# The first normalised tile of an attention and mixture-of-experts kernel: turned by DMA instead of by TensorE

## The chip, the cores and the metric

The kernel runs on one core of one Trainium2 chip. The metric is the time of one execution on the device, in microseconds. Five engines run their own instruction streams and meet only at semaphores: TensorE (PE), VectorE (DVE), ScalarE (ACT), GpSimd (POOL), and SyncE (SP), which here only issues DMA transfers.

## The reference

Layer norm, cross-attention to a short context, layer norm, and a feed-forward block with eight experts and a shared one, both added to their input:

```python
x = x + _L0_xattn_ref(_layernorm(x), ctx_512, Wq, Wkv_expand, Wout)
x = x + _L0_ffn_ref(_layernorm(x), router_w, wg, wu, wd, sg_w, sg_b, su_w, su_b, sd_w, sd_b)
# attention: 16 heads of 32, 64 keys per batch, masked where the key index is above the query's
# feed-forward: two experts per token, chosen and weighted by the router's scores,
#   y = sum over the two of score * (silu(x @ wg) * (x @ wu)) @ wd, plus the shared expert with biases
```

x is 8 batches x 512 tokens x 512, float32.

## The kernel before

The 4096 tokens are T = 32 tiles of 128, four to a batch. The kernel has a fill (loading and scaling of weights, mixed with the first tiles), the passage of the 32 tiles through attention, the shared expert over 32 tiles, and the experts over 71 slots of gathered tokens. The change is in the fill and the passage.

Every matrix that TensorE multiplies is split into two float16 parts, a high and a low one, and a product is three passes (high-high, high-low, low-high). ScalarE makes the high part with a scaled copy, and VectorE or GpSimd the low part as the difference to what was copied.

The passage is a software pipeline. `step(b, j)` on every engine works on tile 4b + j and on the tiles up to six behind it (t1 to t6): first layer norm of the tile itself, turning it (t1), product by w_q and scores (t2), probabilities times values (t3), projection by w_o, residual and second layer norm's statistics (t4), second normalised tile xn2 (t5), router (t6). The order of instructions on each engine is written out by hand in these step functions; nothing reorders them, so an instruction that waits holds all behind it on its engine. The batches 3 to 7 run in a hardware loop; the rest is unrolled. After the last tile six more steps (`LAG`) drain the pipeline, and the shared expert's entries are woven into them (`entry_amid`).

In such a step of tile n, the first layer norm goes: statistics on VectorE (L1057, L1062, `ln_var`); the variance chain `inv_std` on GpSimd, three one-column instructions L566, L569, L573, whose last releases `ln_rstd`; the activation L850 on ScalarE, which writes the float32 tile `xn1` (one buffer). In the step after, TensorE turns xn1 with four float32 transposes into a PSUM bank (`turn_first`, L1417), ScalarE copies the high part into `xn1T` and VectorE makes the low part (`turn_first` in each of them). The second normalised tile goes another way already: ScalarE writes xn2 (L840) and the high part of `xn2p`, GpSimd subtracts the low part (L643), and SP issues a DMA transpose of both into `xn2T` (L446).

Beside this, from batch 2 on, ScalarE and GpSimd split the experts' weights in pieces of 512 columns: ScalarE writes the high part and a scaled float32 copy `piece` (one buffer), and GpSimd subtracts (L580). The steps j = 0, 2 and 3 of a batch have two pieces each, j = 1 has none, but has `batch_keys` on GpSimd (L609, four copies that follow one another); j = 3 has `batch_values` (L617). GpSimd also adds a bias to the residual tile (L668) and joins the router's logits (L659). The splits of w_o, w_r and the shared expert's weights are made in steps 3 to 9 (`more_weights`), the values of the context in pairs of batches (`VALUE_PAIRS`).

Of the kernel before, what the change touches and what calls it, by code (L numbers as in the profile page):

```python
# [25 lines left out]
F16 = mybir.dt.float16  # L26
# [6 lines left out]
P = 128  # L33
# [48 lines left out]
VALUE_PAIRS = ((0, 6, 0), (3, 0, 2), (1, 2, 4), (2, 2, 6))  # L82
VALUE_PARTS = 8
# [5 lines left out]
def xattn_moe(nc, x, ctxT, wqT, wkT, wvT, woT, routerT, experts, shared, sh_b, sd_b, out):  # L89
# [5 lines left out]
    with stack:  # L95
# [70 lines left out]
        silu_g = sb("silu_g", [P, I])  # L166
        hid = sb("hid", [P, I])
# [11 lines left out]
        sums_out = hidT[:, 2:4, :, :, :].rearrange("p n v c q -> p (n v c q)")  # L179
# [58 lines left out]
        def flat(t4):  # L238
# [23 lines left out]
        xn1_ready, xn1T_mm, xn1T_hi, xn1T_ready, q_mm, qT_hi, qT_ready = [sem(n) for n in (  # L262
            "xn1_ready", "xn1T_mm", "xn1T_hi", "xn1T_ready", "q_mm", "qT_hi", "qT_ready")]
# [30 lines left out]
        wo_scaled, wsh_scaled = sem("wo_scaled"), sem("wsh_scaled")  # L294
# [63 lines left out]
        def value_banks(n):  # L358

            first = VALUE_PAIRS[n][1]  # L360
            return (first, first + 1)

        def value_parts(v, n):


            a, z = value_banks(n)
            b = 2 * VALUE_PAIRS[n][0]
            blocks = ((b, a, 2),) if z == a + 1 else ((b, a, 1), (b + 1, z, 1))
            for h in range(2):
                rows = slice(SK * h, SK * h + SK)  # L370
                for first, at, k in blocks:
                    yield rows, v_all[rows, v, first:first + k, :, :], psum[rows, at:at + k, :].rearrange(
                        "p b (r h d) -> p b r h d", h=2, d=HD)[:, :, :, h, :]
# [5 lines left out]
        def _(sp):  # L379
# [28 lines left out]
            def step(b, j):  # L408
                tile = TPB * b + j
                t3, t5, t6 = tile - 3, tile - 5, tile - 6  # L410
# [4 lines left out]
                if live(t3):  # L415
                    load_again(t3, j + 1)
                if live(t6):
# [7 lines left out]
                if j == 2 and isinstance(b, int) and b == 2:  # L425
                    sp.wait_ge(wsh_split, 7)
                    sp.wait_ge(wo_split, 4)
                    sp.wait_ge(wq_split, 2)
                    sp.wait_ge(k_split, 1)
                    sp.wait_ge(v_split, VALUE_PARTS)  # L430
# [1279 lines left out]
```

## Time and profile before

| | us |
|---|---|
| runs | 803.75 median of 3 (800.55 to 804.62) |
| profiled execution | 802.11 |
| its span (first to last instruction) | 800.4 |
| TensorE busy in the span | 762.3 (95%) |
| VectorE, ScalarE, GpSimd busy | 578.3, 459.9, 432.5 |
| first step with pieces to the drain | about 111 to 320 |
| one batch of the loop | 38.0 |

The granted clock of TensorE is a mean of 0.993 of full speed. In a timeline, each row has a start, a duration, the engine, the source line of the profiled kernel, what is written and read with shapes, a count, and, where the engine had been idle before, for how long and who released it. A row of the table by stretch has the stretch, its length, the busy time (and instructions) of PE, PEld (TensorE's weight loads), DVE, ACT and POOL in this order, the granted clock, the busy share of the DMA engines and GB/s. Consecutive equal instructions may be merged into one row. Durations can overlap a little: the next instruction of an engine may start before the last one's end.

### The profile page before, as it was taken

Reading aid. Unit: us, or ns where it says so; the run is one execution under the profiler, and the core shown is the slowest. Engines: PE = TensorE matmul, PEld = TensorE weight load, DVE = VectorE, ACT = ScalarE, POOL = GpSimd, SP = SyncE. Lnnn points to the kernel's source line nnn. Section 1 sums busy time; section 2 is a strip of 40 time slices with the busy share of each in tenths; the row PEclk is TensorE's granted clock in tenths of the full one; section 3 lists DMA queues with packets and bytes.
Section 4 is the critical chain, followed back from the end, with each engine's and each line's share of the span. In section 5 each row is a group of like instructions: output and inputs, shape, how many; then the busy total and the mean of one; then the engine's idle time right before and its main releaser. Section 6 shows DMA issues by size and latency. Waiting matters only on the chain.

```text
span 800.4 us, 21951 instructions
## 1 busy us (share of the span) xinstructions
PE 762.3 (95%) x7249; PEld 522.4 (65%) x7249; DVE 578.3 (72%) x1188; ACT 459.9 (57%) x846; POOL 432.5 (54%) x562
## 2 busy tenths in 40 slices
PE   4888999999999999889999999999999999999995
PEld 2766888888888888668888874455555555555552
DVE  5988999999999898646788685555555565555553
ACT  4777889989888989575546433333333333333330
POOL 3335787777777777444110202655655556556543
PEclk9999999999999999999999999999999999999998
DMA  8325768677766767647856655989898989989892
GB/s 289 121 66 173 205 204 233 191 230 210 207 205 199 215 205 216 200 134 247 266 172 215 195 186 131 138 149 147 145 156 147 160 144 153 152 134 165 145 146 35
DMA packets 138318, 140.73 MB, mean 176 GB/s; under 512 B 87872, under 2 KB 88896, under 8 KB 137856
## 3 DMA queue, kind: packets, MB, share of 16 engines
q1 hardware_dynamic: 122336, 104.01, 47.5%
q0 software_dynamic: 15904, 35.70, 25.6%
q8 instruction: 47, 0.77, 0.4%
q14 instruction: 31, 0.25, 0.1%
HBM read 71.61 MB, written 52.31 MB: 155 GB/s over the span
## 4 chain that ended last, share of the span: by engine, by line
PE 79%; DMA 3%; ACT 1%; issue 1%; POOL 1%; DVE 1%; SPq 0%; POOLq 0%; ACTq 0%
PE psum L1426 45%; PE psum L1489 18%; PE psum L1417 9%; PE psum L1541 4%; PE psum L1580 2%; DMA hidT<-xn2p 1%; DMA out<-w_q,tabs 1%; DMA probsT<-normed_turned 0%; DMA xn1T<-normed_turned 0%; PE psum L1559 0%; PE psum L1601 0%; PE psum L1562 0%; PE psum L1544 0%; ACT attnT L747 0%; ACT xn L840 0%
## 5 line engine op out<-in xcount | busy, mean ns | idle before, releaser
L727 POOL DMA_INDIRECT out<-w_q,tabs x71 | 112.5, 1584 | 108.6 <-DVE w_q L1406 74.3
L717 POOL DMA_INDIRECT x_in<-normed_tokens,tabs x71 | 70.5, 993 | 91.2 <-DVE tabs L1287 42.2
L922 ACT ACTIVATE silu_g<-psum,tabs 128x256 f32<-128x256 f32 x71 | 33.6, 473 | 146.0 <-PE psum L1426 137.8
L1391 DVE SCALAR_TENSOR_TENSOR hid<-psum,tabs,silu_g 128x256 f32<-128x256 f32 x71 | 34.4, 484 | 111.3 <-ACT silu_g L922 111.3
L1426 PE MATMUL psum<-exp_all,hidT 128*128 x426 | 103.4, 379 | 1.7 <-DMA hidT<-xn2p 1.5
L1426 PE MATMUL psum<-exp_all,probsT 128*128 x420 | 96.4, 379 | 0.0
L1426 PE MATMUL psum<-w_o,attnT 128*128 128x512 f16 x384 | 89.7, 384 | 1.6 <-DVE attnT L1111 1.6
L1489 PE MATMUL psum<-xn1T,w_q 128*128 128x128 f16 x1536 | 91.0, 219 | 0.0
L1489 PEld LDWEIGHTS psum<-xn1T,w_q 128*128 128x128 f16 x1536 | 86.3, 98 | 0.7 <-issue 0.6
L580 POOL TENSOR_TENSOR exp_all<-piece,exp_all 128x512 f32 (+1 forms) x48 | 56.2, 1170 | 43.9 <-ACT piece L747 43.9
L1426 PEld LDWEIGHTS psum<-exp_all,hidT 128*128 128x128 f16 x426 | 41.7, 98 | 52.3 <-issue 3.4
L1426 PEld LDWEIGHTS psum<-exp_all,probsT 128*128 128x128 f16 x420 | 41.1, 98 | 41.9
L1406 DVE TENSOR_SCALAR w_q<-psum,y_w 128x512 f32<-128x512 f32 x71 | 53.3, 751 | 20.2 <-PE psum L1426 16.7
L1426 PEld LDWEIGHTS psum<-w_o,attnT 128*128 128x128 f16 x384 | 35.6, 98 | 40.9 <-issue 2.2
L747 ACT ACTIVATE probsT<-psum 128x512 f16<-128x512 f32 x99 | 55.6, 601 | 8.2 <-PE psum L1417 8.0
L1541 PE MATMUL psum<-kv_store,qT 128*128 128x256 f16 x384 | 48.5, 273 | 5.9 <-issue 4.0
L747 ACT ACTIVATE xn2p<-hid 128x256 f16<-128x256 f32 x70 | 29.2, 417 | 38.6 <-DVE hid L1391 37.5
L1426 PE MATMUL psum<-exp_all,qT 128*128 x216 | 49.6, 379 | 0.0
L1426 PE MATMUL psum<-exp_all,xn1T 128*128 x216 | 49.6, 379 | 0.0
L1489 PE MATMUL psum<-probsT,w_sh 128*128 128x128 f16 x768 | 45.8, 219 | 2.4 <-DMA probsT<-normed_turned 1.7
L1489 PEld LDWEIGHTS psum<-probsT,w_sh 128*128 128x128 f16 x768 | 43.8, 98 | 5.0 <-issue 2.9
L1426 PE MATMUL psum<-w_sh,hidT 128*128 128x512 f16 x192 | 46.7, 379 | 0.0
(213 smaller groups left out, 1645.0 us busy)
## 6 DMA issues: line engine op xcount, KB each, us to landing
x_in<-x SPq DMA_DIRECT2D x64, 256.0 KB, 3.0
exp_all<-experts SPq DMA_DIRECT2D x24, 512.0 KB, 5.1
out<-xy SPq DMA_DIRECT2D x32, 256.0 KB, 3.3
normed_tokens<-xn SPq DMA_DIRECT2D x32, 256.0 KB, 4.8
normed_turned<-xn2T SPq DMA_DIRECT2D x32, 256.0 KB, 3.4
w_q<-out SPq DMA_DIRECT2D x32, 256.0 KB, 2.8
out<-w_q SPq DMA_DIRECT2D x32, 256.0 KB, 2.1
probsT<-normed_turned SPq DMA_DIRECT2D x16, 256.0 KB, 3.3
```

What stands on the lines that cost most here:

```text
L580: pool.tensor_tensor(split_piece(e, 1, k), piece[:, :], split_piece(e, 0, k), ALU.subtract).then_inc(piece_split, 1)
L717: pool.indirect_dma_start(x_in[:, t % 4, :], None, xn_dram, bass.IndirectOffsetOnAxis(gather_at[:, t:t + 1], 0)).then_inc(gathered[t % 4], 16)
L727: pool.indirect_dma_start(out, bass.IndirectOffsetOnAxis(add_at[:, t:t + 1], 0), y[:, t % Y_RING, :], None, bounds_check=TOKENS - 1, oob_i ...
L747: act.activation(dst, src, ACT.Copy, scale=scale).then_inc(done, 1)
L922: act.activation(silu_g[:, :], psum[:, GU_BANK[m % 2], 0:I], ACT.Silu, scale=gate_scale_at[:, tm:tm + 1]).then_inc(silu_ready, 1)
L1391: dve.scalar_tensor_tensor(hid[:, :], psum[:, GU_BANK[m % 2], I:2 * I], up_scale_at[:, tm:tm + 1], silu_g[:, :], ALU.mult, ALU.mult).then_ ...
L1406: dve.tensor_scalar(y[:, k % Y_RING, :], bank(DOWN_BANK[k % 2]), y_w[:, tk % 4, :], None, ALU.mult).then_inc(y_ready, 1)
L1417: last = pe.transpose(dst[:, c * P:(c + 1) * P], src[:, c * P:(c + 1) * P], ident[:, :])
L1426: last = pe.matmul(dst, lhsT(a, c), rhs(z, c), start=(c == 0 and a == z == 0), stop=(c == n - 1 and a == 1))
L1489: last = pe.matmul(dst[:, o * P:(o + 1) * P], weights(a, c, o), xT[:, z, c, :], start=(c == 0 and a == z == 0), stop=(c == C - 1 and a == 1))
L1541: last = pe.matmul(dst, qT[:, a, c, :], k_bd[:, z, c, :, :].rearrange("p h k -> p (h k)"), start=(a == z == 0 and (j != 2 or c % 2 == 0)), ...
L1580: last = pe.matmul(dst, probsT[:, a, r, :], v_bd[:, z, r, :, :].rearrange("p h w -> p (h w)"), start=(a == z == 0), stop=(a == 1))
```

## The change

The first normalised tile goes the way of the second. ScalarE, straight behind L850, makes the high part in `xn1p`, GpSimd subtracts the low part (`low_first`, behind the variance chain of the next tile), and SP issues a DMA transpose of both into xn1T (`turn_first`). The transposes on TensorE, the copy from PSUM and VectorE's low part go. xn1p has two buffers, in the space of hidT, which is first used by the shared expert; the throw-away outputs of the absolute sums move to other tiles for that. With it the fill is cut anew: ScalarE makes only the high parts of w_o, w_r and the shared weights, the scaled copy is made by GpSimd in front of its subtraction (`low_weights`), and VectorE takes two pieces of w_o and two of the shared weights; the values are made as one pair for batches 0, 1 and 6, 7 and then one batch per step; the scales of the shared weights are computed over three steps; the first loads of the shared expert's tiles are issued within a step of the drain.

```diff
-VALUE_PAIRS = ((0, 6, 0), (3, 0, 2), (1, 2, 4), (2, 2, 6))
+VALUE_GROUPS = ((0, 6, 2), (6, 0, 2), (2, 6, 1), (3, 6, 1), (4, 6, 1), (5, 6, 1))
...
@@ sync
+            def turn_first(tile, j):
+                sp.wait_ge(xn1_parts, tile + 1)
+                plain(sp)
+                wait(sp, q_mm, tile)
+                plain(sp)
+                sp.dma_start_transpose(xn1T[:, :, :, :].rearrange("p v c q -> p (v c) q"),
+                                       xn1p[:, j % 2, :, :].rearrange("p v h -> p (v h)")).then_inc(xn1_turned, 16)
...
+                if isinstance(tile, int) and tile == T + 1:
+                    load_shared(0)
...
+                if live(t1) and not (isinstance(t1, int) and t1 == 0):
+                    turn_first(t1, j + 1)
...
             load_x(1, 1)
+            turn_first(0, 0)
             sp.dma_start(r_raw, routerT).then_inc(wo_in, 16)
...
@@ gpsimd
+            def low_first(tile, j):
+                pool.wait_ge(xn1_hi, tile + 1)
+                plain(pool)
+                pool.tensor_tensor(xn1p[:, j % 2, 1, :], xn1[:, :], xn1p[:, j % 2, 0, :], ALU.subtract).then_inc(xn1_parts, 1)
...
+            def low_weights(dst, raw, start, size, which, done):
+                here = slice(start, start + size)
+                pool.tensor_scalar(raw[:, here], raw[:, here], inv2[:, which:which + 1], None, ALU.mult).then_inc(w_scaled, 1)
+                scaled_pieces[0] += 1
+                pool.wait_ge(w_scaled, scaled_pieces[0])
+                pool.tensor_tensor(dst[:, 1, here], raw[:, here], dst[:, 0, here], ALU.subtract).then_inc(done, 1)
...
                 if live(tile):
                     inv_std(0, tile)
+                if live(t1) and not (isinstance(t1, int) and t1 == 0):
+                    low_first(t1, j + 1)
...
@@ scalar
-                if live(t1) and not (isinstance(t1, int) and t1 == 0):
-                    turn_first(t1)
...
                 if live(tile):
                     act.wait_ge(ln_rstd[0], tile + 1)
+                    wait(act, xn1_parts, tile)
                     act.activation(xn1[:, :], x_in[:, j % 2, 0:H], ACT.Identity, bias=rstd[:, 0, 2:3],
                                    scale=rstd[:, 0, 1:2]).then_inc(xn1_ready, 1)
+                    act.wait_ge(xn1_ready, tile + 1)
+                    wait(act, xn1_turned, 16 * (tile - 1))
+                    copy(xn1p[:, j % 2, 0, :], xn1[:, :], 1.0, xn1_hi)
...
@@ vector
+                if isinstance(b, int) and (b, j) == (1, 2):
+                    second_scales()
+                if isinstance(b, int) and (b, j) == (1, 3):
+                    third_scales()
...
+                if isinstance(b, int) and (b, j) == (0, 3):
+                    for k in (2, 3):
+                        dve.wait_ge(wo_hi, k + 1)
+                        low_weights(w_o, wo_raw, k, M_WO, wo_split)
...
@@ tensor
-            def turn_first(tile):
-                pe.wait_ge(xn1_ready, tile + 1)
-                wait(pe, xn1T_ready, tile)
-                transposes(bank(7), xn1[:, :], C, xn1T_mm)
...
-                    pe.wait_ge(xn1T_ready, t2 + 1)
+                    pe.wait_ge(xn1_turned, 16 * (t2 + 1))
```

On GpSimd, a step with two pieces (tile 10; ln1 is the first layer norm, ln2 the second) reads before:

```order
L566 TENSOR_SCALAR rstd<-moments 128x1 [waits ln1_var,xn1_ready]
L569 TENSOR_TENSOR rstd<-rstd,minus_half 128x1 [waits ln1_eps]
L573 TENSOR_SCALAR rstd<-moments,rstd 128x1 [waits ln1_pow]
L643 TENSOR_TENSOR xn2p<-xn,xn2p 128x512 [waits xn2_hi]
L580 TENSOR_TENSOR exp_all<-piece,exp_all 128x512 [waits piece_hi]
L659 TENSOR_TENSOR logits<-logit_terms 128x8 [waits terms_ready]
```

and of the change:

```order
L570 TENSOR_SCALAR rstd<-moments 128x1 [waits ln1_var,xn1_ready]
L573 TENSOR_TENSOR rstd<-rstd,minus_half 128x1 [waits ln1_eps]
L577 TENSOR_SCALAR rstd<-moments,rstd 128x1 [waits ln1_pow]
L584 TENSOR_TENSOR hidT<-xn,hidT 128x512 [waits xn1_hi]
L660 TENSOR_TENSOR xn2p<-xn,xn2p 128x512 [waits xn2_hi]
L590 TENSOR_TENSOR exp_all<-piece,exp_all 128x512 [waits piece_hi]
L676 TENSOR_TENSOR logits<-logit_terms 128x8 [waits terms_ready]
```

One subtraction (L584, in the space of hidT) has come in behind the chain; the rest has kept its order. ScalarE in the same step, before:

```order
L747 ACTIVATE xn1T<-psum 128x512 [waits xn1T_mm]
L840 ACTIVATE xn<-xy,rstd 128x512 [waits xn2_stored1,ln2_rstd]
L747 ACTIVATE xn2p<-xn 128x512 [waits xn2_turned,xn2_ready]
L850 ACTIVATE xn<-x_in,rstd 128x512 [waits ln1_rstd]
L747 ACTIVATE logit_terms<-psum,sc 128x16 [waits logits_ready,router_mm]
L747 ACTIVATE exp_all<-exp_all,esc 128x512 [waits e_scales_ready]
L747 ACTIVATE piece<-exp_all,esc 128x512
```

and of the change:

```order
L853 ACTIVATE xn<-xy,rstd 128x512 [waits xn2_stored1,ln2_rstd]
L766 ACTIVATE xn2p<-xn 128x512 [waits xn2_turned,xn2_ready]
L864 ACTIVATE xn<-x_in,rstd 128x512 [waits xn1_parts,ln1_rstd]
L766 ACTIVATE hidT<-xn 128x512 [waits xn1_turned,xn1_ready]
L766 ACTIVATE logit_terms<-psum,sc 128x16 [waits logits_ready,router_mm]
L766 ACTIVATE exp_all<-exp_all,esc 128x512 [waits e_scales_ready]
L766 ACTIVATE piece<-exp_all,esc 128x512
```

The copy out of PSUM at the head is gone, one from xn1 stands behind the activation that writes xn1 (L850, now L864), and that activation has a second semaphore to wait for. SP's first transfers, before:

```order
L382 DMA x_in<-x 128x512
L490 DMA exp_all<-routerT 128x32
L491 DMA exp_all<-woT 128x2048
L492 DMA exp_all<-shared 128x3072
L493 DMA sh_bias<-sh_b 128x4
```

and of the change:

```order
L374 DMA x_in<-x 128x512
L387 DMA_TRANSPOSE xn1T<-hidT 128x8x128 [waits xn1_parts]
L492 DMA exp_all<-routerT 128x32
L493 DMA exp_all<-woT 128x2048
L494 DMA exp_all<-shared 128x3072
```

The loads from the router's on stand behind a transfer that waits for the first tile's parts.

## Rows read from the trace of the kernel before

**Rows 1.** Table by stretch: one batch of the loop.

```profile
196.00:234.00 38.00, 37.98 (x489) 31.03 (x486) 35.45 (x64) 34.35 (x59) 28.74 (x49) 1.00 0.74 214
```

**Rows 2.** Timeline of GpSimd, step of tile 19 (j = 3) and the start of the next.

```profile
195.59 0.19 POOL L566 TENSOR_SCALAR rstd<-moments 128x1 f32<-128x1 f32 x1
...
197.14 0.60 POOL L617 COPY kv_store<-kv_store 64x512 f16 x1 [0.25 <-issue]
...
198.91 1.16 POOL L643 TENSOR_TENSOR xn2p<-xn,xn2p 128x512 f16<-128x512 f32 x1 [0.27 <-POOL kv_store L617]
...
200.03 1.16 POOL L580 TENSOR_TENSOR exp_all<-piece,exp_all 128x512 f32 x1
...
205.18 0.19 POOL L566 TENSOR_SCALAR rstd<-moments 128x1 f32<-128x1 f32 x1
```

**Rows 3.** Timeline of ScalarE, end of step 19 and step of tile 20.

```profile
201.42 0.72 ACT L747 ACTIVATE exp_all<-exp_all,esc  x1 [1.12 <-POOL exp_all L580]
...
205.04 0.84 ACT L840 ACTIVATE xn<-xy,rstd 128x512 f32<-128x512 f32 x1
...
206.54 0.80 ACT L850 ACTIVATE xn<-x_in,rstd 128x512 f32<-128x512 f32 x1
...
207.24 0.25 ACT L747 ACTIVATE logit_terms<-psum,sc 128x16 f32<-128x16 f32 x1
...
208.01 0.71 ACT L747 ACTIVATE piece<-exp_all,esc 128x512 f32 x1
```

**Rows 4.** Timeline of GpSimd, step of tile 20; starts of steps 21 and 22.

```profile
206.21 0.27 POOL L573 TENSOR_SCALAR rstd<-moments,rstd 128x1 f32<-128x1 f32 x1 [0.21 <-POOL rstd L569]
...
209.07 1.17 POOL L580 TENSOR_TENSOR exp_all<-piece,exp_all 128x512 f32 x1 [1.10 <-ACT piece L747]
...
215.03 0.19 POOL L566 TENSOR_SCALAR rstd<-moments 128x1 f32<-128x1 f32 x1
...
224.15 0.19 POOL L566 TENSOR_SCALAR rstd<-moments 128x1 f32<-128x1 f32 x1
```

**Rows 5.** Timeline of TensorE's weight loads, the transposes of xn1 in one step.

```profile
212.99 0.47 PEld L1417 LDWEIGHTS psum<-ident,xn 128*128 128x128 f32 x4
```

**Rows 6.** List of transfers, whole span; queue 1 in the 3.5 us from 200.0.

```profile
xn2T<-xn2p SPq DMA_TRANSPOSE x32, 3.1
...
q1 hardware_dynamic: 1200, 0.27, 41.3%
```

**Rows 7.** Timelines of SP and ScalarE in the fill: wo's load, the sums over it.

```profile
7.87 0.43 SPq L491 DMA_DIRECT2D exp_all<-woT  x1
...
13.38 1.91 ACT L755 ACTIVATE hidT<-exp_all 128x2048 f16<-128x2048 f32 x1 [4.26 <-DMA exp_all<-woT]
```

**Rows 8.** Timeline of GpSimd: waits in step 8; starts of steps 9, 10 and 31.

```profile
96.00 0.20 POOL L659 TENSOR_TENSOR logits<-logit_terms 128x8 f32<-128x8 f32 x1 [1.99 <-ACT logit_terms L747]
...
97.25 0.19 POOL L566 TENSOR_SCALAR rstd<-moments 128x1 f32<-128x1 f32 x1 [1.04 <-DVE moments L1062]
...
99.87 0.19 POOL L566 TENSOR_SCALAR rstd<-moments 128x1 f32<-128x1 f32 x1
...
110.82 0.19 POOL L566 TENSOR_SCALAR rstd<-moments 128x1 f32<-128x1 f32 x1
...
309.53 0.19 POOL L566 TENSOR_SCALAR rstd<-moments 128x1 f32<-128x1 f32 x1
```

**Rows 9.** Timeline of TensorE's weight loads: one wait in step 4, two products after step T+1.

```profile
46.94 1.22 PEld L1541 LDWEIGHTS psum<-kv_store,qT 128*128 128x128 f16 x12 [2.81 <-issue]
...
335.42 4.10 PEld L1489 LDWEIGHTS psum<-xn1T,w_sh 128*128 128x128 f16 x48 [3.46 <-issue]
...
344.87 2.69 PEld L1489 LDWEIGHTS psum<-qT,w_sh 128*128 128x128 f16 x48
```

**Rows 10.** Table by stretch, columns as in rows 1: two microseconds at the lower clock.

```profile
49.00:50.00 1.00, 1.00 (x4) 0.35 (x3) 1.00 (x2) 0.00 (x0) 0.00 (x0) 0.50 0.08 18
336.00:337.00 1.00, 1.00 (x12) 1.00 (x10) 0.00 (x0) 0.00 (x0) 0.24 (x1) 0.50 0.95 363
```

More of the change, by code:

```diff
@@ L436, in step @@
                     to_dram(b - 1)
+                if isinstance(tile, int) and tile == T + 1:
+                    load_shared(1)
                 if live(t5):
@@ L623, in step @@
                 tile = TPB * b + j
-                t2, t3, t4, t5, t6 = [tile - n for n in range(2, 7)]
+                t1, t2, t3, t4, t5, t6 = [tile - n for n in range(1, 7)]
                 e, pieces = pieces_at(b, j)
@@ L670, in step @@
                     low_piece(e, pieces[1])
+                if isinstance(tile, int) and tile == 0:
+                    low_first(0, 0)
             for b in range(3):
@@ L775, in weight_piece @@
                 copy(dst[:, 0, here], raw[:, here], inv2[:, which:which + 1], done)
-                copy(raw[:, here], raw[:, here], inv2[:, which:which + 1], done)
             def more_weights(tile):
@@ L805, in expert_sums @@
                 plain(act)
-                act.activation(sums_out, exp_raw[:, bass.ds(e * WE + start, size)], (ACT.Square, ACT.Square, ACT.Abs)[n],
+                out_here = sums_out
+                if isinstance(e, int) and e == E - 1:
+                    act.wait_ge(xn1_turned, 16 * T)
+                    out_here = xn1p[:, 1, :, :].rearrange("p n w -> p (n w)")
+                act.activation(out_here, exp_raw[:, bass.ds(e * WE + start, size)], (ACT.Square, ACT.Square, ACT.Abs)[n],
                                accum_out=emag[:, n:n + 1]).then_inc(e_mags, 1)
@@ L1119, in step @@
                     expert_scales(scaled, 2)
-                if live(t1) and not (isinstance(t1, int) and t1 == 0):
-                    turn_first(t1)
                 if isinstance(t2, int) and t2 == 0:
@@ L1454, in values @@
             def values(n):
-                for i in range(2):
-                    last = pe.matmul(bank(value_banks(n)[i]), ctx_sb[:, 2 * VALUE_PAIRS[n][0] + i, :, :].rearrange(
-                        "p d k -> p (d k)"), wv_sb, start=True, stop=True)
+                first, at, k = VALUE_GROUPS[n]
+                for i in range(k):
+                    last = pe.matmul(bank(at + i), ctx_sb[:, first + i, :, :].rearrange("p d k -> p (d k)"), wv_sb,
+                                     start=True, stop=True)
                 last.then_inc(v_mm, 1)
@@ L1506, in step @@
                     spread_magnitudes(2)
-                if isinstance(t2, int) and t2 in (1, 2):
-                    pe.wait_ge(shifted, t2)
-                    values(t2 + 1)
-                entry_amid(tile, entry)
+                if isinstance(tile, int) and tile == T + 2:
+                    entry_amid(tile, entry)
                 if live(t4):
@@ L1529, in step @@
                     values(1)
+                if not (isinstance(tile, int) and tile == T + 2):
+                    entry_amid(tile, entry)
                 if live(t2):
                     pe.wait_ge(qT_ready, t2 + 1)
-                    if isinstance(t2, int) and t2 in (1, 2):
-                        pe.wait_ge(v_split, 4 + 2 * t2)
                     wait(pe, shifted, t2)
@@ L1546, in step @@
                     last.then_inc(scores_mm, 1)
+                if isinstance(t2, int) and 0 <= t2 < 4:
+                    pe.wait_ge(v_split, 4 + 2 * t2 if t2 else 2)
+                    values(t2 + 2)
                 if isinstance(b, int) and (b, j) == (1, 1):
```

136 lines of the change are left out of this document (59 added, 77 removed).

## The prediction

> **What bounds the kernel now.** I read three views: the table by stretch, the timelines of GpSimd (POOL), ScalarE (ACT) and the weight loads of TensorE (PEld), and the list of transfers. One batch of the attention loop (four tiles, 38.0 us, 9.5 per tile) has TensorE busy for 37.98 of 38.00 us; VectorE for 35.45, ScalarE for 34.35 and GpSimd for 28.74 [rows 1]. So TensorE is the bound, and what comes off it should pay. But GpSimd's 76% misleads: in the step of tile 19 it goes from one variance chain at 195.59 to the next at 205.18 without an idle stretch beyond its waits for its own results [rows 2]. Where it does idle (1.10 us before a weight piece in the next step), it waits for others [rows 4]. Slack, then, isn't 9 us per batch, and it depends on who waits for whom. I call the work between two starts of the first variance chain (L566) a step.
>
> **What the change takes off.** Per tile TensorE loses four transposes, 0.47 us of its pace [rows 5]. If nothing else moved, a step would take about 9.05 us. VectorE loses one pass over a 128x512 tile, ScalarE swaps a copy from PSUM for one from SBUF.
>
> **What it adds in the loop.** GpSimd gets a 128x512 subtraction per tile. The same form costs 1.16 us and lets the next instruction start after 1.12 [rows 2]. GpSimd alone could about bear this: in the step of tile 20 it still waits for a piece [rows 4]. What it can't bear is the order. The activation that writes xn1 (L850) now also waits for xn1_parts of the tile before, because xn1 is a single buffer that this subtraction still reads; and the subtraction stands on GpSimd *behind* the variance chain of the new tile. Before, the activation started 0.06 us after the chain's end (206.48, then 206.54) [rows 3, 4]. Behind the activation, in order on ScalarE, stand the new copy, the copy of the logits and the two copies of a weight piece; GpSimd's next-but-one instruction waits for that piece. The two engines so form one ring:
> - variance chain, start to end: 205.18 to 206.48 = 1.30 us [rows 2, 4];
> - subtraction: +1.12 = 2.42 [rows 2];
> - to ScalarE: GpSimd's piece ended at 201.19 and ScalarE went on at 201.42, so +0.23 = 2.65 [rows 2, 3];
> - on ScalarE, from L850's start to the piece's end, 206.54 to 208.72 = 2.18. The new copy waits for L850's result as L840's copy does for its own: that pair takes 205.04 to 206.54 = 1.50 where L850 alone holds the engine for 0.70. So 2.18 + 0.80 = 2.98, sum 5.63 [rows 3];
> - back to GpSimd: 208.72 to 209.07, +0.35 = 5.98 [rows 3, 4];
> - piece, logits, second variance chain, addition, second piece, up to the next step: 200.03 to 205.18 = 5.15 [rows 2].
>
> That is **11.13 us for a step with weight pieces**; GpSimd's copies of values or its xn2p subtraction fit within the ScalarE part (2.42 plus 197.14 to 200.03, less the 0.25 us wait at its head, is 5.1, under 5.98) [rows 2]. The step with batch_keys (j = 1) has no piece: 215.03 to 224.15 = 9.12, no slack, +1.12 = **10.24** [rows 4]. The steps of tiles 10 to 30 hold 16 of the first kind and 5 of the second: 178.1 + 51.2 = 229.3 us, where they took 309.53 - 110.82 = 198.71 [rows 8]. **+30.6.** Tile 31 is like tile 19: 11.13 for 9.59, **+1.5**.
>
> TensorE has 2 us of room in such steps. The new transfer must land before the next step's product by w_q: SP issues it at 2.5, it takes 3.1 from issue to landing as xn2T's does [rows 6], so 5.6; product done by 8.3; ScalarE wants it at 8.7 (5.98, piece 1.16, +0.23, two copies). It is hidden, and if it came 2 us later ScalarE's wait for GpSimd would still cover most of that.
>
> The engines of the DMA have room as well: they are busy for 0.74 of a batch, 28 us [rows 1]; an xn2T transpose fills 41.3% of 3.5 us = 1.45 us [rows 6], four more make 34 of now 43.6. The Trainium skill ("DMA: Bandwidth & Descriptors", Latency and other measured facts) gives 261 GB/s for a DMA transpose with a non-contiguous middle dimension, which would be an estimated 1.0 us for these 0.26 MB, 32 us per batch in all; by either the transfers don't bind, and the row decides.
>
> **Tiles 8 and 9.** GpSimd now scales the shared weights itself before it subtracts: two scalings per step more. No row has this form; between a one-column tensor_scalar (0.19 at L566) and a two-input pass (1.16) I take the one-input copy, 0.60 with 0.25 of wait [rows 2], so +0.9 each. Step 8 has 3.03 us of idle time that swallows 1.12 + 1.8; step 9 (10.95, no idle) doesn't: **+2.9**, bounds 1.5 and 4.0 [rows 8]. No idle stretch follows in which GpSimd could catch up.
>
> **The fill.** The first transpose stands in SP's queue ahead of the loads of router, wo and shared. It waits for GpSimd's first subtraction, by the same latencies at 9.4, and holds SP until 10.7; wo is issued at 11.2 instead of 7.87, and ScalarE's sums wait for it (13.38 is its landing) [rows 7]: about +3.3 there, +2.5 at the first scores. The subtraction of tile 1 stands behind batch_keys and tile 2's variance chain, so the second product by w_q starts some 3 us later still, mostly given back because ScalarE no longer scales wo twice and the values are spread over four steps. Against it: ScalarE's long stretch behind which TensorE idled for 2.81 us until 46.94 goes, with it probably the stretch at half clock that followed [rows 9, 10], and six steps shed up to 0.5 each: about -4. Sum **-1.5**, bounds -5 and +5.
>
> **The passage to the shared expert.** Its first load is issued inside step T+1 instead of behind it; TensorE stood for 3.46 us before 335.42 and then worked at 1.2 GHz, 4.10 us for 48 matmuls that take 2.69 [rows 9, 10]. Both go: -4.9; transposes now stand ahead of the expert's product one step later, -0.4. **-5.3.**
>
> **Sum:** +30.6 + 1.5 + 2.9 - 1.5 - 5.3 = +28.2. The profiled execution took 802.11 us, so 830.3; it lies 1.6 under the median of 803.75, so **832**. A measurement can tell about 0.5% (4 us) from no change.
>
> **Rivals.**
> 1. *GpSimd's throughput alone* (chance 0.08). If ScalarE weren't held at L850, because GpSimd runs ahead, a batch would cost GpSimd its 38.0 us less the 4.2 in which it waits for others, plus 4.5: 38.3, +0.3 per batch, +1.6; 1.6 + 2.9 - 1.5 - 5.3 = -2.3: 801. Against it: GpSimd has no idle stretch in steps 19 and 21 in which to run ahead [rows 2, 4].
> 2. *TensorE stays the bound* (0.07), the other side. The wait is satisfied in time and TensorE's 0.45 us per tile counts: 22 steps give -10, and -1.5 + 1 - 5.3: 788. It decides from where the subtraction ends before ScalarE gets to L850; with 0.06 us between them now, 1.35 us would have to be found.
> 3. *TensorE at half clock too* (0.13). In 11.13 us steps it idles 2 us, perhaps in one piece before the product by w_q. Here the granted clock fell to 0.50 (1.2 GHz) after stretches of 2.81 and 3.46 us, and not after shorter ones [rows 9, 10]. If the transfer lands 1 us late in every step, that product takes 4.1 instead of 2.7 or more and the end of it passes into ScalarE's slack and beyond: about 1 us per step, +22: 854. The Trainium skill ("TensorE: Matmul & The Clock Gate", The HAM clock gate) tells of such a loop, where a wait for a transfer in each round drops the clock in each round; by it this would be the case here, and the rows leave it open.
> 4. *Forecast* (0.72): 832, own bounds 820 to 844 (0.3 us per step is 6.6, the fill 5).
>
> **How the numbers follow.** The range takes in my case and the nearer part of rival 3 and leaves out rivals 1 and 2 (0.15): 812 to 852. Faster by over 0.5%: rival 2 and part of 1 and of the unforeseen, 0.10; within: 0.07; slower: 0.83.
>
> **What would show it.** Right: steps with pieces of 11.1 us and j = 1 steps of 10.2 between starts of the first variance chain; ScalarE's xn1 activation waiting 1 to 3 us for GpSimd's subtraction in each; GpSimd waiting for the piece; TensorE busy for about 83% of the loop, with granted clock 1.00. Wrong: a step under 9.8, an activation that doesn't wait, or a loop in which TensorE waits for xn1T.

## The result, and the profile after

The change makes the kernel slower: 856.87 us median (855.78 to 860.65, four runs) against 803.16 us for the kernel before, a ratio of 1.068 (95% interval 1.065 to 1.071). The profiled execution took 857.8 us, its span 854.4 (before: 802.1 and 800.4). The direction of the forecast holds, and so does its mechanism for the steps with weight pieces. The size does not: 832 was said, with 812 to 852 as the range. Above all, the new transfer, which the forecast called hidden, lands late once per batch, and TensorE's clock falls during the wait; and the fill lost time where a gain was forecast.

The starts of the first variance chain (now L570) divide the added 54.0 us of span into three parts:

| | before | after | difference | forecast |
|---|---|---|---|---|
| start of tile 10's step | 110.82 | 121.08 | +10.3 | +1.4 |
| tiles 10 to 30 | 198.71 | 240.17 | +41.5 | +30.6 |
| tile 31's step to the end | 490.87 | 493.15 | +2.3 | -3.8 |

**The ring is there.** GpSimd in the step of tile 20 and the one behind it, to be held against [rows 2, 4]:

```profile
235.68 0.19 POOL L570 TENSOR_SCALAR rstd<-moments 128x1 f32<-128x1 f32 x1
...
236.93 1.15 POOL L584 TENSOR_TENSOR hidT<-xn,hidT 128x512 f16<-128x512 f32 x1
238.04 1.16 POOL L660 TENSOR_TENSOR xn2p<-xn,xn2p 128x512 f16<-128x512 f32 x1
241.48 1.16 POOL L590 TENSOR_TENSOR exp_all<-piece,exp_all 128x512 f32 x1 [2.27 <-ACT piece L766]
...
246.61 0.19 POOL L570 TENSOR_SCALAR rstd<-moments 128x1 f32<-128x1 f32 x1
...
252.30 1.16 POOL L660 TENSOR_TENSOR xn2p<-xn,xn2p 128x512 f16<-128x512 f32 x1 [3.28 <-ACT xn2p L766]
...
260.16 0.19 POOL L570 TENSOR_SCALAR rstd<-moments 128x1 f32<-128x1 f32 x1
```

ScalarE in the same time (the activation that writes xn1 is L864 now):

```profile
238.19 0.81 ACT L864 ACTIVATE xn<-x_in,rstd 128x512 f32<-128x512 f32 x1 [1.19 <-POOL hidT L584]
...
248.44 0.60 ACT L766 ACTIVATE qT<-psum 128x512 f16<-128x512 f32 x1 [4.25 <-PE psum L1509]
```

The subtraction holds GpSimd for 1.11 us, ScalarE waits 1.19 us for it, and GpSimd then waits 2.27 us for the weight piece. The step takes 246.61 - 235.68 = 10.93 us; the sixteen steps with pieces between tile 10 and 31 take 174.9 us, 10.93 on average, where 11.13 was forecast.

**What the ring doesn't hold** is the next step, the one with batch_keys: 13.55 us here, and 15.00, 12.24, 12.51 and 12.00 in the other batches, 65.3 in all, where 51.2 was forecast. SP and then TensorE (matmuls) around it:

```profile
234.80 0.35 SPq L406 DMA_DIRECT2D mag_rows<-magnitudes  x1
235.43 0.34 SPq L374 DMA_DIRECT2D x_in<-x  x1
236.04 0.33 SPq L379 DMA_DIRECT2D x_in<-x  x1
236.67 0.36 SPq L422 DMA_DIRECT2D normed_turned<-xn2T  x1
237.23 0.36 SPq L426 DMA_DIRECT2D out<-xy  x1
238.32 1.30 SPq L387 DMA_TRANSPOSE xn1T<-hidT  x1
```

```profile
243.10 5.30 PE L1509 MATMUL psum<-xn1T,w_q 128*128 128x128 f16 x48 [3.22 <-DMA xn1T<-hidT]
```

The transpose is issued at 238.32, as soon as GpSimd's part is ready, but the product starts at 243.10, 4.8 us later and not 3.1. TensorE has then idled for 3.22 us, and the product takes 5.30 us where its pace at 2.4 GHz gives 2.85: the granted clock has fallen to 0.50 (1.2 GHz), as the table by stretch shows for these 5.30 us:

```profile
243.10:248.40 5.30, 5.30 (x49) 5.30 (x50) 0.18 (x1) 1.10 (x2) 4.65 (x8) 0.50 1.04 305
```

ScalarE waits 4.25 us for that product and GpSimd 3.28 us for ScalarE. One batch in the table by stretch (columns as in rows 1):

```profile
213.87:257.87 44.00, 37.77 (x453) 30.28 (x452) 31.56 (x57) 32.68 (x55) 31.10 (x50) 0.92 0.76 203
```

TensorE is busy for 86% of it, even with slow products counted as busy, and the clock is 0.92 on average, where it was 1.00 [rows 1]. For the whole span, the page's group of these matmuls (32 tiles with 48 each; busy us, mean ns of one, idle time before them, what ended it):

```profile
L1509 PE MATMUL psum<-xn1T,w_q 128*128 128x128 f16 x1536 | 105.5, 236 | 45.2 <-DMA xn1T<-hidT 43.7
```

In the page of the kernel before, the same group has no idle time:

```profile
L1489 PE MATMUL psum<-xn1T,w_q 128*128 128x128 f16 x1536 | 91.0, 219 | 0.0
```

The steps with pieces also have a wait of TensorE for xn1T, of 0.9 to 1.8 us in two of three. It lies within the 2 us of room that the forecast gave them, and the clock stays up there.

### The profile page after: what moved, and what is told of

It is laid out like the page before. It is cut to its first block, busy times and chain, and to the rows that moved or that the text cites. A ratio compares the mean times of both kernels' runs of the same rounds, so it can differ in the third digit from the quotient of the medians.

```text
span 854.4 us, 21861 instructions
## 1 busy us (share of the span) xinstructions
PE 770.0 (90%) x7121; PEld 520.9 (61%) x7121; DVE 569.7 (67%) x1164; ACT 458.2 (54%) x839; POOL 471.8 (55%) x597
## 4 chain that ended last, share of the span: by engine, by line
PE 51%; POOL 10%; DMA 9%; issue 7%; ACT 5%; SPq 1%; POOLq 1%; DVE 1%; ACTq 0%; DVEq 0%
PE psum L1452 34%; PE psum L1509 12%; PE psum L1443 4%; DMA xn1T<-hidT 4%; POOL rstd L573 2%; POOL hidT L584 2%; DMA out<-w_q,tabs 2%; POOL exp_all L590 2%; DMA hidT<-xn2p 2%; POOL kv_store L624 1%; POOL xy L685 1%; ACT piece L766 1%; ACT xn L864 1%; DMA magnitudes<-emag 1%; POOL rstd L570 1%
## 5 line engine op out<-in xcount | busy, mean ns | idle before, releaser
L1509 PE MATMUL psum<-xn1T,w_q 128*128 128x128 f16 x1536 | 105.5, 236 | 45.2 <-DMA xn1T<-hidT 43.7
L1509 PEld LDWEIGHTS psum<-xn1T,w_q 128*128 128x128 f16 x1536 | 100.1, 107 | 49.5 <-DMA xn1T<-hidT 42.2
L938 ACT ACTIVATE silu_hid<-psum,tabs 128x256 f32<-128x256 f32 x71 | 33.6, 473 | 146.5 <-PE psum L1452 146.5
L1417 DVE SCALAR_TENSOR_TENSOR silu_hid<-psum,tabs,silu_hid 128x256 f32<-128x256 f32 x71 | 34.4, 484 | 111.8 <-ACT silu_hid L938 111.8
L1452 PEld LDWEIGHTS psum<-exp_all,hidT 128*128 128x128 f16 x426 | 41.5, 98 | 52.9 <-issue 3.9
L987 DVE SCALAR_TENSOR_TENSOR qT<-psum,qT 128x512 f16<-128x512 f32 x32 | 22.0, 688 | 69.9 <-ACT qT L766 69.8
L766 ACT ACTIVATE qT<-psum 128x512 f16<-128x512 f32 x50 | 29.7, 594 | 53.9 <-PE psum L1509 47.2
L660 POOL TENSOR_TENSOR xn2p<-xn,xn2p 128x512 f16<-128x512 f32 x32 | 37.1, 1161 | 24.0 <-ACT xn2p L766 22.1
L766 ACT ACTIVATE xn2p<-silu_hid 128x256 f16<-128x256 f32 x70 | 29.2, 417 | 38.6 <-DVE silu_hid L1417 38.6
```

What stands on the lines that cost most here:

```text
L660: pool.tensor_tensor(xn2p[:, 1, :], xn2[:, (j + 1) % 2, 0:H], xn2p[:, 0, :], ALU.subtract).then_inc(xn2_parts, 1)
L766: act.activation(dst, src, ACT.Copy, scale=scale).then_inc(done, 1)
L938: act.activation(silu_g[:, :], psum[:, GU_BANK[m % 2], 0:I], ACT.Silu, scale=gate_scale_at[:, tm:tm + 1]).then_inc(silu_ready, 1)
L1417: dve.scalar_tensor_tensor(hid[:, :], psum[:, GU_BANK[m % 2], I:2 * I], up_scale_at[:, tm:tm + 1], silu_g[:, :], ALU.mult, ALU.mult).then_ ...
L1452: last = pe.matmul(dst, lhsT(a, c), rhs(z, c), start=(c == 0 and a == z == 0), stop=(c == n - 1 and a == 1))
L1509: last = pe.matmul(dst[:, o * P:(o + 1) * P], weights(a, c, o), xT[:, z, c, :], start=(c == 0 and a == z == 0), stop=(c == C - 1 and a == 1))
```

## The experiments

All start from the kernel after. e1 to e7 and e9 try one repair each, e8 is built on e2, and the last three put several together. The table gives the run's median, the ratio to the kernel before with its interval, and from the profiled execution the start of tile 10's step, the time from there to tile 31's, and the rest of the span.

| | us | ratio | tile 10 | 10 to 31 | rest |
|---|---|---|---|---|---|
| before | 800.7 to 804.7 | 1 | 110.8 | 198.7 | 490.9 |
| after | 856.9 | 1.068 (1.065-1.071) | 121.1 | 240.2 | 493.2 |
| e1 two buffers | 844.8 | 1.055 (1.051-1.058) | 121.6 | 229.3 | 491.0 |
| e2 on VectorE | 829.9 | 1.036 (1.033-1.038) | 122.8 | 215.0 | 490.4 |
| e3 busy TensorE | 847.4 | 1.058 (1.056-1.060) | 121.1 | 229.4 | 492.6 |
| e4 magnitudes behind | 871.9 | 1.088 (1.086-1.090) | 123.6 | 248.7 | 498.7 |
| e5 ScalarE scales | 854.9 | 1.066 (1.063-1.068) | 121.5 | 233.9 | 497.3 |
| e6 first turn later | 852.8 | 1.065 (1.060-1.070) | 117.7 | 239.4 | 494.6 |
| e7 entries first | 852.2 | 1.062 (1.059-1.065) | 121.8 | 239.6 | 490.5 |
| e8 xn1 in PSUM | 825.0 | 1.031 (1.027-1.035) | 118.3 | 211.3 | 491.0 |
| e9 magnitudes next step | 849.1 | 1.055 (1.051-1.060) | 121.9 | 229.2 | 498.1 |
| e10 all in one | 821.6 | 1.020 (1.015-1.025) | 116.3 | 212.1 | 493.0 |
| e11 = e9 + e5 | 842.3 | 1.053 (1.047-1.059) | 116.2 | 226.9 | 495.8 |
| e12 repaired | 832.5 | 1.038 (1.033-1.042) | 116.5 | 222.5 | 495.4 |

The rest of the span moves by some us between kernels that are alike there, so differences of a few us in that column prove nothing.

**Is it the ring?** e1 gives xn1 a second buffer (to make room for it, three small tables for the experts move into other tiles):

```diff
-                    wait(act, xn1_parts, tile)
-                    act.activation(xn1[:, :], x_in[:, j % 2, 0:H], ACT.Identity, bias=rstd[:, 0, 2:3],
+                    wait(act, xn1_parts, tile - 1)
+                    act.activation(xn1_two[:, j % 2, :], x_in[:, j % 2, 0:H], ACT.Identity, bias=rstd[:, 0, 2:3],
```

> The xn1 tile gets two buffers, so ScalarE's xn1 activation waits for the subtraction of two tiles ago instead of the tile before; nothing else moves. Ring theory (GpSimd's chain and subtraction, then ScalarE's activation, copies and piece, then GpSimd's rest): the 1.2 to 1.4 us wait at that activation goes, the steps with weight pieces fall from 10.9 to about 9.9 us, the steps with batch_keys stay at about 13, total about 838 us (16 such steps in the loop and a few in the fill, 1.0 each). Rival, TensorE's wait for the transfer and its half clock set every step: steps stay at 10.9 and the total within 3 us of 857.

```profile
256.78 0.81 ACT L866 ACTIVATE xn<-x_in,rstd 128x512 f32<-128x512 f32 x1 [0.26 <-POOL rstd L578]
```

This is ScalarE's activation in the step of tile 22: it waits only for the variance chain. The third step of a batch takes 9.73 us, the first about 10.1, the last (with batch_values) 10.65, where all took 10.9 to 11.15. So the wait for the single buffer is real and worth 0.3 to 1.2 us per step. The batch_keys steps took 14.3, 13.0, 11.4, 13.3 and 11.4 us; the waits for xn1T before their products are 3.64, 2.69, 2.65, 3.01 and 2.62 us, and the two that took 11.4 are those in which the product ran at 2.4 GHz (2.85 us; 4.43 to 5.30 in the others). The total came out 7 us over what I expected. About half of that is one step with pieces of 14.05 us, ahead of which a further product came late (3.77 us of wait, 5.30 us for the product at the lower clock); the rest is that most steps shrank by less than the 1.0 us expected.

**Is it the clock?** e3 lets TensorE work while it waits, in the batch_keys steps of batches 3 to 7:

```diff
+                if j == 1 and live(t2) and not isinstance(b, int):
+                    for i in range(13):
+                        pe.matmul(bank(7), w_o[:, 0, 0:P], w_o[:, 0, 0:H], start=True, stop=True)
```

> In the batch_keys steps of batches 3 to 7 TensorE runs 13 matmuls of 128x512 on data that nobody reads (into the bank that the change left free) ahead of its wait for xn1T, about 3.0 us at full clock, where it now idles 3.2 us. Clock theory: the product by w_q then runs at 2.4 GHz, 2.7 us instead of 5.0, and the five steps shrink by 2.3 us each: about 845 us. Rival, the late landing alone sets those steps and the half clock is covered by ScalarE's slack: product at 2.7 us but steps unchanged, total 857.

TensorE in the step of tile 21:

```profile
235.78 2.75 PE L1518 MATMUL psum<-w_o 128*128 128x512 f16 x12
238.86 2.85 PE L1509 MATMUL psum<-xn1T,w_q 128*128 128x128 f16 x48 [0.32 <-DMA xn1T<-hidT]
```

From the issue at 234.19 to the product it is 4.7 us, as late as before, but the product runs at 2.4 GHz, and the batch_keys steps fall to 12.8, 10.5, 10.8, 10.5 and 10.3. From tile 10 to 31 it takes 229.4 us, 10.8 less. So most of what the late landing costs, it costs by the clock. That the time is now my 229.3 is a coincidence: the batch_keys steps take 54.9 us in all, of 65.3 in the kernel after and 51.2 in the forecast, so the clock explains 10.4 of their 14.1 us too much, and the 3.6 that stay are offset by steps with pieces that are shorter than forecast. Extra work on an idle engine made the kernel 8 us faster.

**Why does it land late?** In e4 the load of the experts' magnitudes (`from_dram`, once per batch) is issued behind the transpose instead of at the head of SP's step:

```diff
-                if j == 0 and found(b - 2) is not None:
-                    from_dram(b - 2)
...
                     turn_first(t1, j + 1)
+                if j == 0 and found(b - 2) is not None:
+                    from_dram(b - 2)
```

> On SP the load of the experts' magnitudes (192 KB, once per batch) goes from the head of the step to just behind the transpose of xn1p; all else as after. Theory that the transpose of that step lands late because five transfers stand ahead of it in the same rings: it lands about 0.6 us earlier (4.2 instead of 4.8 us after its issue), the batch_keys steps shrink by 0.6 us, or by up to 3 where the shorter wait also keeps the clock up: 853, at best 843. Rival, the landing depends on what is issued behind it or on the transpose itself: no change, 857, or slower because VectorE gets the magnitudes later.

Slower by 15 us. All five batch_keys steps take 10.23 to 10.25 us, as forecast (10.24), but the steps ahead of them 15.1 to 15.8 instead of 11.1. VectorE, and then TensorE, in the step of tile 20:

```profile
249.67 0.66 DVE L1089 TENSOR_REDUCE emax<-mag_rows 128x3 f32<-128x384 f32 x1 [5.61 <-DMA mag_rows<-magnitudes]
```

```profile
246.53 2.85 PE L1509 MATMUL psum<-xn1T,w_q 128*128 128x128 f16 x48 [1.59 <-DMA xn1T<-hidT]
252.72 0.66 PE L1443 MATMUL psum<-ident,attn 128*128 128x128 f32 x4 [3.33 <-DVE attn L1200]
253.22 1.78 PE L1443 MATMUL psum<-ident,probs 128*128 128x128 f32 x8
```

VectorE reads the magnitudes in its order, ahead of the residual, waits 5.61 us for them, and TensorE 3.33 us for VectorE; the transposes of the probabilities then take 1.78 us for 1.04. The stall had changed its place. So e9 moves reader and load: the load to the end of SP's first step, VectorE's reduction to the step behind:

```diff
                 if scaled is not None:
+                    expert_scales(scaled, 0)
+                    expert_scales(scaled, 1)
                     expert_scales(scaled, 2)
```

> The load of the experts' magnitudes is issued at the end of SP's first step of a batch instead of at its head, and VectorE reads it in the batch_keys step (behind the probabilities' low parts) instead of in the first; all else as after. The earlier run that moved only the load showed batch_keys steps of 10.2 us, as I had priced them, but paid 4.3 us in the first step, where VectorE waited for it. Theory that this one transfer, in front of the transpose, makes the late landing and through it the half clock: first steps 11.1, batch_keys steps 10.3 to 10.6 (VectorE's chain of short instructions is in one piece now), the loop from tile 10 to 31 takes 229 to 232 us instead of 240.2, and tile 10 starts 2 to 4 us earlier; total 842 to 847. Rival, the five transfers as a whole or SP's own issue time make it late: batch_keys steps stay above 11.5 and the total above 852.

SP and TensorE in the step of tile 20:

```profile
235.49 1.25 SPq L387 DMA_TRANSPOSE xn1T<-hidT  x1
```

```profile
238.65 2.85 PE L1506 MATMUL psum<-xn1T,w_q 128*128 128x128 f16 x48 [1.63 <-DMA xn1T<-hidT]
```

Without the 192 KB ahead of it, the transpose is followed by its product after 3.16 us, my 3.1. TensorE idles for 1.63 us, and the clock stays up. The load now stands behind the transpose, and nothing else in SP's queue ahead of it has changed; as e4 moved the load alone and had the same batch_keys steps, it is the load that made the landing late. Steps: 10.7 to 11.0 with pieces, 10.25 to 10.26 in four of five batch_keys steps (13.63 in the first batch, after a wait of 2.70 us and a product of 4.48). Tiles 10 to 31 take 229.2 us, within the 229 to 232 expected of this run (that the prediction said 229.3 is the same coincidence as in e3). Two things didn't come as expected: tile 10 started no earlier, and some of the gain was lost in the drain, where TensorE waited for a tile of the shared expert and worked at 1.2 GHz again:

```profile
420.52 4.47 PE L1506 MATMUL psum<-probsT,w_sh 128*128 128x128 f16 x48 [2.86 <-DMA probsT<-normed_turned]
```

**The fill.** e5 lets ScalarE scale the pieces that GpSimd subtracts:

```diff
             def low_weights(dst, raw, start, size, which, done):
-                pool.tensor_scalar(raw[:, here], raw[:, here], inv2[:, which:which + 1], None, ALU.mult).then_inc(w_scaled, 1)
...
             def weight_piece(dst, raw, start, size, which, done, scale_too):
+                if scale_too:
+                    copy(raw[:, here], raw[:, here], inv2[:, which:which + 1], w_scaled)
```

> In the fill ScalarE again scales the pieces of w_o, of the router and of the shared weights that GpSimd subtracts (one copy more per piece there), so GpSimd's seven scalings of about 1.6 us, of which I had priced four at 0.9 us, are gone. Theory that these scalings make most of what the fill lost beyond my sum: the steps of tiles 8 and 9 shrink by about 3 us each where GpSimd had no slack, tile 10 starts at 116 to 118 us instead of 121.1, total about 853. Rival, the fill waits for the transpose and for TensorE at 1.2 GHz: tile 10 still starts at 120 or later, total within 2 us of 857.

Nothing at tile 10: 121.5. GpSimd's step 9 in the kernel after has no wait over 0.26 us; it is full with its own work:

```profile
108.04 1.57 POOL L597 TENSOR_SCALAR exp_all<-exp_all,inv 128x512 f32<-128x512 f32 x1
109.69 1.16 POOL L600 TENSOR_TENSOR w_sh<-exp_all,w_sh 128x512 f16<-128x512 f32 x1
```

In e5 the same step has another limit. TensorE and GpSimd there:

```profile
105.00 5.30 PE L1510 MATMUL psum<-xn1T,w_q 128*128 128x128 f16 x48 [4.77 <-DMA xn1T<-hidT]
```

```profile
114.04 1.16 POOL L659 TENSOR_TENSOR xn2p<-xn,xn2p 128x512 f16<-128x512 f32 x1 [4.00 <-ACT xn2p L765]
```

Two paths of about equal length: GpSimd's scalings, and the late transpose with the product at 1.2 GHz. e9 removed the late transpose ahead of step 9 alone (2.02 us of wait before 101.50, product in 2.85 us), and step 9 kept its 15.5 us; e5 removed the scalings alone, and it took 16.1. e11 is both edits:

> The two edits of the fill that alone moved nothing at tile 10 together: the magnitudes a step later, and the weights scaled by ScalarE again. Theory of two paths of about equal length in the steps of tiles 8 and 9, one through the late transpose and the half clock, one through GpSimd's own work (its two scalings per step, 1.65 us each with their wait): only with both gone do the steps shrink; tile 9's from 15.5 to about 12.3, tile 10 starts at 116 to 118 us where it started at 121.9 and 121.5 with one, total about 845. Rival, ScalarE's added copies are as long as the scalings they replace: tile 10 still at 120 or later, total 849.

Step 9 takes 12.05 us, which is the 10.95 of the kernel before and 1.12 for the subtraction, and tile 10 starts at 116.2. Neither edit moved it, both together by 4.9 us. The loop runs at full clock (table by stretch, one batch, columns as in rows 1):

```profile
203.19:246.18 42.99, 37.33 (x468) 29.19 (x467) 34.43 (x60) 34.80 (x59) 33.07 (x53) 1.00 0.80 212
```

e6 puts the first transpose behind the loads of router and wo:

> The first transpose stands on SP behind the loads of the router and of wo instead of ahead of them. Theory from my working: wo is there 3.3 us earlier, the first steps and with them everything start 1.5 to 2.5 us earlier, total about 855. Rival: the start is set by VectorE's magnitudes and splits, nothing moves: 857.

SP and ScalarE; in the kernel after, wo was issued at 11.35 and summed from 16.64 (before: rows 7):

```profile
7.99 0.43 SPq L492 DMA_DIRECT2D exp_all<-woT  x1
```

```profile
13.57 1.91 ACT L776 ACTIVATE probs<-exp_all 128x2048 f16<-128x2048 f32 x1 [5.92 <-DMA exp_all<-woT]
```

Tile 2 starts 2.4 us earlier, tile 8 and tile 10 3.3 us earlier. The edit is worth more than I expected of it, because the delay at the start is not given back. The ratio's interval still overlaps that of the kernel after; the starts in the trace show the gain, the total alone doesn't.

**The drain.** e7 restores the old order of TensorE, entries ahead of attn's transposes (`tile == T + 2` becomes `tile >= T + 2` at two places):

> In the steps that drain the pipeline TensorE takes the shared expert's entry ahead of the transposes of attn in every step from T+2 on, as the kernel before did, and not only in step T+2. Theory that the new order leaves TensorE idle 3.1 us before the transposes at 403 us and sends the product behind it to 1.2 GHz: that gap and 1 us of the product go, the stretch from tile 31's chain to the end falls from 493.2 to 489 to 491 us, total about 854. Rival: attn's transposes then stand behind the entry and delay x1, no gain or up to 2 us slower.

TensorE after, then in e7:

```profile
403.04 1.12 PE L1443 MATMUL psum<-ident,attn 128*128 128x128 f32 x4 [2.97 <-DVE attn L1200]
403.95 3.71 PE L1509 MATMUL psum<-probsT,w_sh 128*128 128x128 f16 x48
```

```profile
399.66 2.84 PE L1509 MATMUL psum<-probsT,w_sh 128*128 128x128 f16 x48 [1.68 <-DMA probsT<-normed_turned]
```

The 2.97 us gap and the slow product are gone, a shorter gap has come. The rest of the span is 490.5 for 493.2, as expected, but that column varies by as much, and the ratios' intervals all but touch (1.0646 and 1.0647): likely, not shown.

**Would VectorE have been the better place?** e2 moves the subtraction there, ahead of the low part of q:

```diff
@@ gpsimd
-                if live(t1) and not (isinstance(t1, int) and t1 == 0):
-                    low_first(t1, j + 1)
...
@@ vector
                     join_stats(0, tile)
+                if live(t1) and not (isinstance(t1, int) and t1 == 0):
+                    low_first(t1, j + 1)
```

> The subtraction that makes the low part of the first normalised tile stands on VectorE (ahead of its low part of q) and not on GpSimd; the DMA transpose, and all else of the change, stays. Theory that GpSimd's place in the ring is the cost of the loop: steps with pieces back to 9.3 to 9.6 us, the transpose issued over 1 us earlier, so the batch_keys steps fall from 13 to about 10.5; total about 805 us. Rival, the transfer with what it brings (late landing, 1.2 GHz) is the cost whoever subtracts: total over 830 us, and TensorE still waits 2 us or more for xn1T in every batch.

```profile
212.69 1.81 DVE L1068 TENSOR_TENSOR hidT<-xn,hidT 128x512 f16<-128x512 f32 x1
```

Most steps take 9.1 to 10.45 us, and the kernel 26 us less (by the ratios) than with the subtraction on GpSimd, though 25 more than expected. Tiles 10 to 31 take 25.1 us less: 18.5 of them in the batch_keys steps (46.8 us in all for 65.3), in which GpSimd sheds its 1.12 us and TensorE waits at most 1.05 us for xn1T, and 6.7 in the steps with pieces. So the largest single cause is that GpSimd makes the subtraction, and more of it lies in the batch_keys steps than in the ring. But VectorE's pass takes 1.81 us, while GpSimd's addition runs from 212.67 to 213.95, and GpSimd's next subtraction takes 1.62 for 1.16. In the batch_keys step of the same run, where GpSimd has no 128x512 instruction until the pass is over, the same instruction takes 0.69 us:

```profile
243.55 0.69 DVE L1068 TENSOR_TENSOR hidT<-xn,hidT 128x512 f16<-128x512 f32 x1
```

```profile
244.34 1.27 POOL L677 TENSOR_TENSOR xy<-xy,sd_bias 128x512 f32<-128x512 f32 x1
```

In e8, besides, ScalarE writes the tile to a PSUM bank from tile 4 on, and VectorE reads it there:

> As the run with VectorE's subtraction, but from tile 4 on the normalised tile lies in a PSUM bank, so VectorE's subtraction has one operand there and not both in SBUF. In the run with both in SBUF it took 1.81 us where its other passes of that size take 0.68, and stood ahead of q's low part, for which TensorE waited 1.2 us. Theory that this is contention with GpSimd over SBUF: the subtraction takes 0.7 us, the steps fall from 10.2 to 9.2 to 9.5 us, total about 810 us. Rival, the transfers or ScalarE's extra copy hold those steps at 10.2 or more: within 5 us of 830.

```profile
207.85 0.69 DVE L1072 TENSOR_TENSOR hidT<-psum,hidT 128x512 f16<-128x512 f32 x1
```

0.69 us beside the same addition of GpSimd. The Trainium skill ("SBUF — State Buffer", Who interferes with whom) says that a VectorE instruction with two SBUF inputs contends with a GpSimd instruction that reads SBUF. The three passes agree: 1.81 us with both inputs in SBUF beside GpSimd's addition, 0.69 with both there and no such instruction beside it, 0.69 with one in PSUM. Most steps with pieces came down only to 9.66 to 9.96 us, not to 9.5, and the total only to 825.0 where 810 was expected: ScalarE's new copy still stands in the loop between ScalarE and GpSimd (that it holds these steps is argued, not shown), and TensorE still waited for xn1T once per batch (3.06 us before 185.92, 2.12 before 225.95).

e10 puts together e8, e9, e6 and e7, with ScalarE's copy behind the weight piece and the transpose at the head of SP's step:

> All that the runs so far point to, put together: the normalised tile in PSUM and its low part by VectorE, ScalarE's copy of its high part behind the weight piece (out of the ring with GpSimd), the transpose at the head of SP's step in batches 3 to 7, the magnitudes a step later, the first transpose behind the loads of router and wo, the shared expert's entries ahead of attn's transposes in the drain. If the transpose was hard to hide only for these reasons, TensorE is the bound again and gives its 0.47 us per tile: steps of 9.0 to 9.5 us, total 790 to 803. Rival, with the copy from SBUF the loop of ScalarE and GpSimd still holds the steps at 9.6 or more: total 805 to 815.

The best of all at 821.6 us, but outside both expectations. From the second of its batches on, the first steps take 9.2 to 9.8 us, the last 9.6 to 10.3, the batch_keys steps 9.15 to 9.95; the third steps take 10.8 to 10.9, for 9.4 before, which makes 8.7 of the 13.4 us that tiles 10 to 31 take more than in the kernel before. There GpSimd waits for VectorE's statistics of the second layer norm:

```profile
285.79 0.19 POOL L577 TENSOR_SCALAR rstd<-moments 128x1 f32<-128x1 f32 x1 [1.52 <-DVE moments L1085]
```

What holds that step I did not test. e12 keeps the subtraction on GpSimd and has the edits of e1, e9, e5, e6 and e7:

> GpSimd keeps the subtraction; all that the runs named is repaired beside it: two buffers for the normalised tile, the magnitudes a step later, the scaling on ScalarE, the first transpose behind router and wo, the entries first in the drain. If the causes are separate they add up to about 857 - 12 (two buffers) - 8 (magnitudes) - 4 (first transpose) - 4 (drain) - 4 (scaling) = 825, with loop steps of 9.7 to 10.7 and no stretch at 1.2 GHz in the loop. Rival, they hide one another: total over 835.

832.5 us, 7 over the sum: three of the five batch_keys steps take 11.05 instead of 10.25 when the others are shorter, the first takes 13.98, with 2.56 us of wait and a product of 4.48 us, and step 9 takes 14.8 instead of 12.05, behind a wait of 2.10 us for xn1T and another product of 4.48 us. So the lower clock is not gone, and the repairs don't simply add up. No version beats the kernel before.

## Why the prediction was right or wrong, point by point

- **The bound and the ring: right.** Steps with pieces 10.93 us (11.13 said), with the two waits in their places; e1 shows that the single buffer makes the first of them.
- **The batch_keys step, 10.24 us: right as GpSimd's work, wrong as the step.** e4 and e9 measure 10.24 and 10.26. In the kernel after it is 13.1 on average, 14.1 us more in the five steps than the sum had. The step of the prediction that failed is "It is hidden": I took the landing time of xn2T's transpose (3.1) for a transfer that has up to five others ahead of it in the same queue, looked at their mean over the span, and let 2 us of room stand. In the first step of a batch it took 4.8, of which 1.6 are the load of the magnitudes ahead of it (e4, e9). I also wrote that 2 us more would be covered by ScalarE's wait; the wait isn't there in the batch_keys step. And a sign that the prediction itself named for being wrong, a loop in which TensorE waits for xn1T, is what the trace shows.
- **Rival 3: right in kind, wrong in how often.** I saw that a gap before the product by w_q could cost the clock, and gave it 0.13 because I asked whether it happens in every step. It happens once per batch: a wait of 2.6 to 4.9 us and a product of 4.2 to 5.3. e3 prices the clock at 10.8 us in this stretch. The rival's 854 is near the result by the chance of its 22 times 1 us, not by its working. The Trainium skill ("TensorE: Matmul & The Clock Gate", HAM oscillation) describes such a loop, with a drop in every round; this trace agrees that waits for a transfer do it, but has one drop per four tiles.
- **The scaling on GpSimd: mis-sized.** 0.9 us was taken, between 0.19 and 1.16; it is 1.57, and 1.65 with its wait. The upper end was a two-input pass, and a one-input scaling turned out to be longer than that. Step 9 by my sum with 1.65 is 10.95 + 1.12 + 3.3 = 15.4; it took 15.46. Step 8 is 10.50 + 1.12 + 3.3 less its 3.03 of idle time, 11.9; it took 11.99. Together +6.0 us, where +2.9 was said.
- **The fill: wrong sign in the sum.** -1.5 us was said for the stretch up to tile 8; tile 8 starts at 93.63 for 89.37, +4.3. The delay in wo's load was found and priced rightly (+3.3), but only 2.5 was carried to the first scores and gains of 4 us were set against it. e6 shows 3.3 us at tile 8 and at tile 10: nothing of it was given back. The idle stretch before 46.94 did shrink (2.00 us before 47.75), with no lower clock behind it, but a new one came, 3.02 us of wait for the second tile's xn1T before 34.38 with 4.14 us for its product. Without the delay of wo (e6) tile 8 still starts 0.9 us later than before, not earlier.
- **The passage: half.** The gap before the shared expert's first product is gone (389.19 starts without a wait), but at 378.5 TensorE waits 2.2 us for xn1T and needs 4.46 for the product by w_q, and the new order brings a gap of 2.97 at 403. I counted the gap that the change removes and not those that its new order makes. That these two gaps make the whole miss of 6.1 us is not shown.

Sum of the misses in the span: 10.9 in the loop (14.1 in the batch_keys steps, less 3.2 in those with pieces, forecast too long), 8.9 in the fill, 6.1 from tile 31 on, together 25.9; with the 28.2 of the forecast that is the 54.0 of the span, to rounding.

## What to carry to other kernels

A transfer that is to be hidden is costed at the worst place of the period, with what stands ahead of it in its queue there, not at its mean. If its consumer is TensorE, a gap of 2 to 3 us can cost twice: once as the wait, once as the following work at 1.2 GHz. And a step that one edit doesn't move may have two limits of the same length: try the two edits together before either is called harmless.

## What the runs showed of the hardware

- In the kernel after, the product by w_q ran at 1.2 GHz, in whole or for the most part (granted clock 0.50 to 0.67), after all of TensorE's waits for xn1T of 2.23 us or more (2.23, 2.64, 3.02, 3.22, 3.26, 3.39, 4.92, 4.96), and at 2.4 GHz after those of up to 1.78. But e1 kept the higher level after 2.62 and 2.65 us, e8 after 3.06, while e12 lost it after 2.10: between 2.1 and 3.1 us the length of the wait alone doesn't decide. Matmuls on data that nobody reads kept it up (e3), for a gain of 8 us.
- A load of 192 KB in 1.5 KB rows ahead of a transpose in SP's queue delayed the transpose by 1.6 us (4.8 against 3.16 from issue to the product that waited for it).
- A 128x512 float32 scaling by a per-partition factor takes GpSimd 1.57 us, more than its two-input subtraction of that size (1.16).
- VectorE's subtraction with both inputs in SBUF took 1.81 us beside a 128x512 addition of GpSimd, 0.69 with no such instruction beside it, and 0.69 beside that addition with one input in PSUM.
